# Sharing out nine taps among three engines in a patch-filter layer

## The reference, cut to what matters

```python
y = einsum('oc,bchw->bohw', w_in, x)                # 48 -> 288 channels
yp = y in patches of 8 x 8
y = irfft2(rfft2(yp) * fft_mask)                    # a filter inside each patch
y = conv(y, w_dw, 3x3, padding 1, one filter per channel)
x1, x2 = split(y, 2)                                # 144 channels each
g = gelu(x1) * x2
out = einsum('oc,bchw->bohw', w_out, g)             # 144 -> 48 channels
```

## Time and profile before

| | |
|---|---|
| time of three runs | 7460.11, 7465.26, 7467.92 us, median 7465.26 us |
| profiled execution | 7462.4 us, of which the profile's span is 7460.1 us |
| the layer that is changed | 3126.9 to 3628.2 us of the span, 501.3 us |
| busy in that stretch | TensorE 445.9 us, VectorE 447.4 us, ScalarE 174.5 us |
| iteration of a band, in the steady part | 28.58 us |

### The profile page before, as it was taken

One profiled execution on the slowest core, in us unless ns is written; L12 is line 12 of the kernel. 1 busy time (PEld: TensorE's weight loads), 2 busy tenths in 40 slices (PEclk: granted clock), 3 DMA queues, 4 the chain that ended last, 5 costly groups with the idle time before them and its releaser, 6 DMA issues. The chain is left out here.

```text
span 7460.1 us, 169553 instructions
## 1 busy us (share of the span) xinstructions
PE 6090.7 (82%) x68803; PEld 2679.5 (36%) x69312; DVE 6843.6 (92%) x6229; ACT 5240.9 (70%) x5318; POOL 3429.0 (46%) x1801
## 2 busy tenths in 40 slices
PE   6899999999999999899767777777777777766330
PEld 3333333333333333366323333333333333333220
DVE  7799999999999999899789999999999999986776
ACT  3388888888888888633468888888888888842000
POOL 2000000000000000000169999999999999974777
PEclk9899999999999999999889999999999999987665
DMA  2200000000000000000110000000000000022333
GB/s 42 61 8 8 8 11 8 8 8 8 8 8 11 8 8 8 4 6 7 35 46 6 6 6 6 6 6 6 6 6 6 6 6 6 6 56 74 83 83 82
DMA packets 130880, 146.51 MB, mean 20 GB/s; under 512 B 52524, under 2 KB 111692, under 8 KB 129244
## 3 DMA queue, kind: packets, MB, share of 16 engines
q1 hardware_dynamic: 104160, 82.28, 4.0%
q0 software_dynamic: 24576, 50.36, 2.6%
q10 hardware_dynamic: 1440, 3.75, 0.3%
HBM read 98.55 MB, written 37.75 MB: 18 GB/s over the span
## 5 line engine op out<-in xcount | busy, mean ns | idle before, releaser
L1790 POOL TENSOR_TENSOR k_image<-k_image,s_b 128x1024 f32<-128x1024 f32 x1152 | 2700.8, 2355 | 118.1 <-ACT k_image L1703 83.5
L710 ACT ACTIVATE att_prob<-att_scores,a_bound,a_temp 128x1024 f32<-128x1024 f32 x2048 | 2357.0, 1202 | 420.8 <-PE att_scores L653 420.8
L721 DVE TENSOR_TENSOR att_prob_lo<-att_prob 128x1024 f16<-128x1024 f32 x2048 | 2429.0, 1238 | 139.4 <-ACT att_prob L710 123.0
L638 POOL TENSOR_TENSOR k_image<-k_image,att_rden 48x512 f32 x32 | 67.7, 2116 | 2990.4 <-DVE att_rden L733 2990.4
L1703 ACT COPY k_image<-h_du 128x1024 f32<-128x1024 f32 x1152 | 1166.4, 1013 | 322.9 <-PE h_du L1637 322.3
L1753 DVE TENSOR_TENSOR_SCAN h_state_odd<-h_keep,k_image 128x1024 f32<-128x1024 f32 x576 | 1378.4, 2509 | 0.0
L653 PE MATMUL att_scores<-att_queries,att_keys 32*128 32x512 f16 (+1 forms) x20480 | 1294.0, 377 | 21.5 <-DMA att_queries<-qk_halves 18.8
L1709 ACT ACTIVATE h_keep<-h_keep,h_decay 128x1024 f32<-128x1024 f32 x1152 | 1256.7, 1091 | 74.7 <-PE h_keep L1626 51.2
L670 PE MATMUL att_sums<-att_prob,a_values 128*64 128x512 bf16 x8192 | 1124.9, 395 | 0.0
L1626 PE MATMUL h_keep<-h_rows,h_spread 128*128 128x512 bf16 x2303 | 699.0, 385 | 510.6 <-DVE h_state_odd L1753 263.1
L653 PEld LDWEIGHTS att_scores<-att_queries,att_keys 32*128 32x128 f16 (+1 forms) x20480 | 439.7, 93 | 776.2 <-ACT att_prob L710 379.3
(11 more groups left out here) (295 smaller groups left out, 7021.1 us busy)
## 6 DMA issues: line engine op xcount, KB each, us to landing
y_rows<-h_y_sb SPq DMA_DIRECT2D x1024, 3.0 KB
att_queries<-qk_halves SPq DMA_DIRECT2D x124, 128.0 KB, 2.2
parts<-t_part SPq DMA_DIRECT2D x48, 192.0 KB, 2.5
h_rows<-parts SPq DMA_DIRECT2D x128, 72.0 KB
b_shared<-cells,b_index POOLq DMA_INDIRECT x512, 2.6
qk_halves<-qkv_hi SPq DMA_DIRECT2D x128, 48.0 KB, 1.6
cells<-b_shared SPq DMA_DIRECT2D x4, 1536.0 KB, 5.1
att_keys<-qk_halves SPq DMA_DIRECT2D x32, 128.0 KB, 2.7
```

The lines of the kernel that those rows point to most:

```text
L710: nc.scalar.activation(prob[:, u % RING, :], scores[:, u % SLOTS_S, :], ACT.Exp, bias=bound[:, 0:1], scale=temp[:, 0:1]).then_inc(prob_rea ...
L721: nc.vector.tensor_tensor(prob_lo[:, u % RING, :], prob[:, u % RING, :], prob_hi[:, u % RING, :], ALU.subtract).then_inc(low_ready, 1)
L1790: nc.gpsimd.tensor_tensor(drive[k % 3], du_sb[k % 3], b[:, c * CH:(c + 1) * CH], ALU.mult).then_inc(drive_ready, 1)
```

## The change

ScalarE computes tap 0 of a, b and c for a band (`first_taps`), as soon as the band is placed and joined, and VectorE keeps taps 1 to 8; each of the three accumulators has a semaphore of its own (`first_a`, `first_b`, `first_c`) on which tap 1 waits. TensorE sums five of the eight rows of a instead of six, so that `ps_m` has 128 columns and VectorE's part of a 384. VectorE's masks of half 1 stand after tap 5 and one count instead of after tap 6 and both counts. TensorE's nine taps are in six places of a band instead of three: 0, 1 and 2, 3 and 4 in half 0, and 5 and 6, 7 and 8 in half 1, the third place being new and between the second and the third mixing matmul.

```diff
@@
...
 TAPS = 9
+LATER = TAPS - 1
 PLACES = 6
...
 GELUS = 3
-PE_ROWS = 6
+PE_ROWS = 5
 MID = (PE_ROWS - HALF) * W
 TURN_AT = MIX
-TAPS_BESIDE = ((range(0, 2), range(2, 4)), (range(0), range(4, TAPS)))
+TAPS_BESIDE = ((range(0, 2), range(2, 4), range(4, 5)), (range(5, 6), range(6, 8), range(8, TAPS)))
@@
...
                                "inverted", "placed", "halo"))
-        conv_a, tap_a, tap_b, tap_c, gelu_a, gelu_c, gated, product, added, counted = (
-            n.sem(s) for s in ("conv_a", "tap_a", "tap_b", "tap_c", "gelu_a", "gelu_c", "gated", "product", "added",
+        conv_a, tap_a, tap_b, tap_c, first_a, first_b, first_c, gelu_a, gelu_c, gated, product, added, counted = (
+            n.sem(s) for s in ("conv_a", "tap_a", "tap_b", "tap_c", "first_a", "first_b", "first_c", "gelu_a", "gelu_c", "gated", "product", "added",
                                "counted"))
@@
...
                                      stop=True).then_inc(mixed, 1)
+                    if conv and t == 1:
+                        depthwise(r - 1, 1 - ph, TAPS_BESIDE[hf][2])
                 for b, c0 in ((0, 0), (1, P)):
@@
...
                 wait_past(act, conv_a, k + 1)
-                wait_past(act, tap_a, (k + 1) * TAPS)
+                wait_past(act, tap_a, (k + 1) * LATER)
...
                 nc.scalar.copy(slab_a[:, ph, 0:2, :], slab_a[:, 1 - ph, SLAB - 2:SLAB, :]).then_inc(halo, 1)
-                wait_past(act, tap_b, (r - 1) * TAPS)
+                wait_past(act, tap_b, (r - 1) * LATER)
                 nc.scalar.copy(slab_b[:, ph, 0:2, :], slab_b[:, 1 - ph, SLAB - 2:SLAB, :]).then_inc(halo, 1)
-                wait_past(act, tap_c, (r - 1) * TAPS)
+                wait_past(act, tap_c, (r - 1) * LATER)
                 nc.scalar.copy(slab_c[upper, ph, 0:2, :], slab_c[lower, 1 - ph, HALF:HALF + 2, :]).then_inc(halo, 1)
@@
...
+            def first_taps(r, ph):
+
+                act.wait_ge(placed, r * PLACES + PLACES)
+                act.wait_ge(halo, r * HALOS + HALOS)
+                wait_past(act, gated, 2 * (r - 1))
+                for first, acc, slab, w, row0, nrow in ((first_c, acc_c, slab_c, dwc, 0, HALF),
+                                                        (first_a, acc_a, slab_a, dwa, PE_ROWS, PATCH - PE_ROWS),
+                                                        (first_b, acc_b, slab_b, dwb, 0, PATCH)):
+                    nc.scalar.activation(acc[:, ph, 0:nrow, :], slab[:, ph, row0:row0 + nrow, 0:W], ACT.Copy,
+                                         scale=w[:, 0:1]).then_inc(first, 1)
+
             def gelus_pe(k):
@@
...
             def gelus_dve(k, ph):
-                act.wait_ge(tap_a, k * TAPS + TAPS)
+                act.wait_ge(tap_a, k * LATER + LATER)
                 wait_past(act, product, k)
...
             def gelus_c(k, ph, bases=(0, 64), ncol=BLK):
-                act.wait_ge(tap_c, k * TAPS + TAPS)
+                act.wait_ge(tap_c, k * LATER + LATER)
                 wait_past(act, product, k)
@@
...
                 if hf == 0:
-                    wait_past(act, tap_b, (r - 1) * TAPS)
+                    wait_past(act, tap_b, (r - 1) * LATER)
                 place(r, hf, ph, 1)
                 if hf == 0:
-                    wait_past(act, tap_c, (r - 1) * TAPS)
+                    wait_past(act, tap_c, (r - 1) * LATER)
                 place(r, hf, ph, 2)
...
                     join(r, ph)
+                    first_taps(r, ph)
@@
...
         def _(dve):
-            def tap(sem, acc, slab, w, k, t, ph, row0, nrow):
-
-                if t > 0:
-                    dve.wait_ge(sem, k * TAPS + t)
+            def tap(sem, first, acc, slab, w, k, t, ph, row0, nrow):
+
+                if t == 1:
+                    dve.wait_ge(first, k + 1)
+                else:
+                    dve.wait_ge(sem, k * LATER + t - 1)
                 src = slab[:, ph, row0 + t // 3:row0 + t // 3 + nrow, t % 3:t % 3 + W]
                 out = acc[:, ph, 0:nrow, :]
-                if t == 0:
-                    ins = nc.vector.tensor_scalar(out, src, w[:, t:t + 1], None, ALU.mult)
-                else:
-                    ins = nc.vector.scalar_tensor_tensor(out=out, in0=src, scalar=w[:, t:t + 1], in1=out,
-                                                         op0=ALU.mult, op1=ALU.add)
-                ins.then_inc(sem, 1)
-
-            def tap_c_rows(k, ph, t, nrow=HALF):
-                if t == 0:
-                    dve.wait_ge(placed, k * PLACES + PLACES)
-                    dve.wait_ge(halo, k * HALOS + 4)
-                    wait_past(dve, gated, 2 * (k - 1))
-                    wait_past(dve, gelu_c, 2 * (k - 1))
-                tap(tap_c, acc_c, slab_c, dwc, k, t, ph, 0, nrow)
+                nc.vector.scalar_tensor_tensor(out=out, in0=src, scalar=w[:, t:t + 1], in1=out, op0=ALU.mult,
+                                               op1=ALU.add).then_inc(sem, 1)
+
+            def tap_c_rows(k, ph, t):
+                tap(tap_c, first_c, acc_c, slab_c, dwc, k, t, ph, 0, HALF)
             def tap_a_rows(k, ph, t):
-                if t == 0:
-                    wait_past(dve, gelu_a, GELUS * (k - 1))
-                tap(tap_a, acc_a, slab_a, dwa, k, t, ph, PE_ROWS, PATCH - PE_ROWS)
+                tap(tap_a, first_a, acc_a, slab_a, dwa, k, t, ph, PE_ROWS, PATCH - PE_ROWS)
             def tap_b_rows(k, ph, t):
-                tap(tap_b, acc_b, slab_b, dwb, k, t, ph, 0, PATCH)
+                tap(tap_b, first_b, acc_b, slab_b, dwb, k, t, ph, 0, PATCH)
@@
...
                 dve.wait_ge(gelu_a, GELUS * k + (GELUS if ncol > BLK else 1))
-                dve.wait_ge(tap_b, k * TAPS + TAPS)
+                dve.wait_ge(tap_b, k * LATER + LATER)
                 nc.vector.tensor_tensor(gate_a[:, 0:ncol], gate_a[:, 0:ncol],
...
                 dve.wait_ge(gelu_c, 2 * k + (2 if ncol > BLK else 1))
-                dve.wait_ge(tap_c, k * TAPS + TAPS)
+                dve.wait_ge(tap_c, k * LATER + LATER)
                 m = min(ncol, BLK)
@@
...
                 k, kph = r - 1, 1 - ph
-                for t in range(2):
-                    taps(k, kph, t)
+                taps(k, kph, 1)
                 if out:
@@
...
                         add(r - 2, hh)
-                for t in range(5, 7):
-                    taps(k, kph, t)
+                taps(k, kph, 5)
+                if out and (not isinstance(r, int) or r > 2):
+                    count((r - 2) * 2 - 1)
+                mix(r, 1)
                 if out:
-                    if not isinstance(r, int) or r > 2:
-                        count((r - 2) * 2 - 1)
                     count((r - 2) * 2)
-                mix(r, 1)
-                for t in range(7, TAPS):
+                for t in range(6, TAPS):
                     taps(k, kph, t)
@@
...
                     iteration(i * 2 + ph, ph)
-            for t in range(TAPS):
+            for t in range(1, TAPS):
                 taps(NPR - 1, 1, t)
@@
...
             dve.wait_ge(made, 4 + TAPS)
-            for t in range(TAPS):
-                tap(tap_b, acc_b, slab_b, dwb, NPR, t, 0, 0, 1)
-                tap(tap_c, acc_c, slab_c, dwc, NPR, t, 0, 0, 1)
+            for first, acc, slab, w in ((first_b, acc_b, slab_b, dwb), (first_c, acc_c, slab_c, dwc)):
+                nc.vector.tensor_scalar(acc[:, 0, 0:1, :], slab[:, 0, 0:1, 0:W], w[:, 0:1], None, ALU.mult).then_inc(first, 1)
+            for t in range(1, TAPS):
+                tap(tap_b, first_b, acc_b, slab_b, dwb, NPR, t, 0, 0, 1)
+                tap(tap_c, first_c, acc_c, slab_c, dwc, NPR, t, 0, 0, 1)
             gates(NPR, 0, W)
...
             count(2 * NPR - 1)
```

## The result

The changed kernel takes 7480.32 us (median of 19 runs, 7474.49 to 7483.05) where the kernel before takes 7466.39 (19 runs, 7460.11 to 7470.91): 14 us more, a ratio of 1.0018 with a 95% interval of 1.0011 to 1.0024. The forecast was 7465 with a range of 7456 to 7473. The direction was not foreseen. The profiled execution has a span of 7472.2 us, 12.1 more than the one before.

The account below looks back on a forecast made before the run. VectorE was taken to set the pace. 28.33 + 0.15 = 28.48 us per iteration, 0.10 less, times 14 is -1.4; +1.2 first, -0.25 last: -0.45 us, so 7465 us, range 7456 to 7473.

Parts of the forecast that it names:

- the clock falls: Rival: idle before half 0's third matmul drops TensorE to 1.2 GHz; 182 us for the whole way, 7647 us; chance 0.02.
- the way to half 1: TensorE from half 0's third mixing matmul to half 1's: 15.46 us before, 12.9 to 13.3 after, against VectorE's 12.93.
- the scan layer's row: Evidence against the clock falling: in the scan layer TensorE is busy 157.72 of 200 us at clock 1.00.
- VectorE's own terms: VectorE per iteration: 1.32 us removed with tap 0, 1.07 added by wider taps of a, giving 28.33 from 28.58.
- Moving the masks and one count costs nothing by itself: VectorE's loop: the new places of half 1's masks and one count add 0 us.
- TensorE's lateness: Half 1's third mixing matmul, now behind tap 8, comes 0 to 0.3 us late; 0.15 us of VectorE waiting taken.
- ScalarE's first taps: Three ScalarE operations behind the join, 0.72, 0.61 and 1.16 us; VectorE's new wait on them costs nothing.
- The handover: VectorE's 0.49 us idle before each half's third mask stays; rival that both vanish: 18 us less, 7447, chance 0.02.
- The first iteration: TensorE sets the pace in iteration 1; the inserted tap loses between 0 and 2.4 us, 1.2 taken.
- the last iteration and the end: The last band's taps on VectorE are 0.25 us shorter.

Follow-up runs that it names:

- tap 5 moved: Changed kernel with tap 5 moved from half 1's first place to half 0's third, beside tap 4: 7466.84 us against 7466.51 for the kernel before.
- six rows: Changed kernel with six rows of a on TensorE again instead of five: 7468.58 us against 7466.51 for the kernel before.
- one filler: Changed kernel with one extra unread 256-column matmul ahead of half 0's third mixing matmul: 7456.21 us against 7459.75 for the kernel before.
- counts together: Changed kernel with the second count moved ahead of half 1's masks, beside the first: 7623.56 us against 7626.53 for the kernel before.
- The balanced version: Changed kernel with six rows on TensorE, first taps behind next half's staging, counts and one c tap before half 1's masks: 7440.11 us against 7459.75 for kernel before.

## Why the prediction was wrong

**The step that failed** is the weighing of the rival "the clock falls", at 0.02: the forecast's sum takes TensorE's clock as 1.00 throughout and so puts this term at nothing, where it measured 11.5 us. The text placed it rightly (the idle time of some 2.2 us ahead of the third matmul of half 0, 1.98 measured), named the way to half 1 as the one on which every microsecond costs, and put the point of decision at 1.07 us of it in each of 14 iterations, or 15 us. Measured are 8 falls in 14 iterations at 1.44 us. A fall lasts 3.4 us, not the whole way of 13. I set it aside by the scan layer's row, TensorE busy 79% at a clock of 1.00. That row is a share, and the rival was about a single wait. The waits view of the same 200 us, which I did not set beside it, has the longest wait at 1.1 us:

```profile
PE h_keep L1626 <- DVE h_state_odd L1753: 18.5, 39, 1.1
```

So that row says nothing of a wait of 2 us. Other stretches of the trace of before, on which the prediction does not draw, do. In the attention layer TensorE works at 1.00, waits 2.71 us, and 0.8 us after it has started again the clock is at 0.50 for 3.4 us (two rows of its timeline, then the windows view around the fall):

```profile
96.76 4.05 PE L182 MATMUL qkv_ps_qk<-qkv_x_split,qkv_qk_split 112*112 112x512 f16 x18
103.52 1.26 PE L510 MATMUL qkv_ps_n<-qkv_sq,qkv_ones 112*112 112x512 f32 x2 [2.71 <-DVE qkv_nrm L468]
...
64.00:104.29 40.29, 33.60 (x184) 17.58 (x182) 30.04 (x22) 21.09 (x15) 2.77 (x2) 1.00 0.07 21
104.29:107.70 3.41, 3.41 (x17) 1.25 (x16) 3.38 (x2) 0.60 (x1) 0.00 (x0) 0.50 0.07 19
107.70:290.00 182.30, 179.07 (x1065) 95.19 (x1062) 158.29 (x150) 37.09 (x63) 0.00 (x0) 1.00 0.14 41
```

The same stretch has a wait of 2.28 us and one of 1.70 with no fall behind them. In the first part of the scan layer (3644 to 3783 us) TensorE has twelve waits of 1.55 to 1.67 us, and two of them have such a fall behind them (at 3732.65 and 3770.20). So the trace did not exclude the rival: of the two waits over 2 us in that first stretch one had a fall behind it. A chance near one half would have followed. A fall of 3.4 us at half speed costs at most 1.7 us, so my estimate from these rows would have been up to 12 us if half of the 14 iterations had one and up to 24 if all had.

The experiments show what takes the step's place. Over the kernels of this study, TensorE's longest waits and the falls go together: 1.2, 1.3, 1.4 and 1.5 us with no fall (tap 5 moved, six rows, one filler, counts together), 1.98 with falls in 7 or 8 of 13 windows, 2.36 in 8, 2.8 in 11, 3.1 and 3.6 in all but the first. This order holds for the patch filter's loop. Where falls begin elsewhere it does not say: two waits of some 1.66 us brought one in the scan layer's first part, where TensorE is less busy (68 of the 82 us from 3650). The Trainium skill ("TensorE: Matmul & The Clock Gate", the section on HAM oscillation), which the prediction cited for this rival, does tell of gaps that lower the clock. The runs agree in kind, with falls behind waits of 1.98 us in 7 or 8 of 13 windows.

**VectorE's own terms** held. The taps of a take 611 ns against 479, 0.13 more as worked out. Removed first taps and widened ones together gave the 28.33 of the forecast: it is the 28.32 us of the run with the counts together. "Moving the masks and one count costs nothing by itself" was wrong by 0.24 us per iteration. A count behind a tap starts 0.1 us late and takes 0.72 us from start to start (3407.76 to 3408.48), and doing so twice costs more than the pair's 1.32.

**TensorE's lateness** in half 1, taken at 0.15 us in a range of 0 to 0.3, was 0. The two errors nearly cancel, which is luck: 28.57 us for an undisturbed iteration where 28.48 was forecast. That the way had no slack was right, and it is why a fall surfaces almost whole. In the kernel before, made to fall by leaving out a tap, half 1's 0.42 us of cover took part of it: 1.2 us per fall.

**ScalarE's first taps** take 0.72, 0.60 and 1.13 us where 0.72, 0.61 and 1.16 were forecast. In an undisturbed iteration VectorE does not wait for them, no further table is loaded, and TensorE waits 0.7 to 0.8 us for the transposed copy where 1 was forecast. **The handover** of 0.49 us in either half stayed, as argued, in every undisturbed iteration. **The first iteration** lost 0.75 us (the gates of iteration 2 begin at 3186.93, 2.39 us into it, so it begins at 3184.54 for 3183.79 before), where 1.2 was taken.

The sum with the measured terms: +0.75; +0.3 for iteration 2, which lasts 28.54 us for 28.22 before and for which the forecast had no term of its own; the others at no difference; 8 x 1.44 = 11.5; and -0.2 for the last iteration and the end. That is 12.3 us, against 12.1 between the spans and 12 to 14 between the medians. Without the falls it is 0.9 us, well inside the forecast's range.

**The gain that was to be had** was in the other direction. The change gives TensorE less (25.6 of 28.57 us) and VectorE stays the pace at 27.3 busy. The balanced version keeps six rows on TensorE, takes VectorE's busy time to 26.1, and fills TensorE: 27.37 us. That is shown as a whole only; of its edits the six rows alone (28.72) and the counts alone (28.32) were run by themselves, the move of the first taps behind the staging was not.

## What to carry to other kernels

When an edit makes an engine that was waiting wait longer, and the engine is TensorE, the wait is not free: look for its longest single wait, not its busy share, and keep it no longer than waits that the trace of the same loop shows to be harmless, by spreading work into it or, failing that, with a filler. Where two engines hand work to and fro, add up each engine's way between the handovers; a disturbance on a way without slack shows in full. A row that shows a share says nothing of the length of one gap. Look through the whole trace for a stretch that has such a gap before setting the rival aside; here it was there, in another layer. A rival that no row excludes deserves a real chance.

## What the runs showed that was not expected

- Less work made the kernel slower, which the prediction did not foresee and the expectations by then did: a tap left out in the kernel before cost 9.4 us, and three matmuls without use took away the changed kernel's loss (7468.4 us against 7480).
- The fall is not regular. The same wait of 1.98 us, with the same work around it, was followed by a fall in 7 of 13 windows in one execution and 8 of 13 in another.
- After waits of 3.1 to 3.6 us some falls are longer: the clock over the iteration is 0.90 instead of 0.95, and such an iteration 1.1 to 1.4 us longer than its neighbours.
- Two statistics instructions in a row cost VectorE 0.24 us less than the two with other work between them.
